# Local attention in blocks of 32 queries: paired transposes and values on array quarters

## The reference

```
def local_attention(q, k, v):            # window w = 32, 16 heads of 64
    bq, bk, bv = (t.reshape(b, h, n // w, w, d) for t in (q, k, v))
    bk2, bv2 = look(bk), look(bv)        # each block with the one before it
    mask = (it < jb) | (it > jb + w) | (jb == -1)
    sim = einsum('bhwie,bhwje->bhwij', bq, bk2) * 8.0
    sim = where(mask, -max, sim)
    return einsum('bhwij,bhwje->bhwie', softmax(sim, -1), bv2)

def attn_layer(x, Wqkv, qs, ksc, Wo):
    q, k, v = split(x @ Wqkv, 3, -1)
    q, k = l2norm(q) * qs, l2norm(k) * ksc    # then rotary, with scales
    return local_attention(q, k, v) @ Wo
```

## Time and profile before

| | |
|---|---|
| time, median of 3 runs | 5304.71 us (5301.19 to 5307.71) |
| span of the profiled execution | 5297.4 us, first to last instruction |
| time of the profiled execution itself | not listed apart from the three runs |
| instructions | 148317 |
| TensorE, VectorE, ScalarE, GpSimd busy | 88%, 76%, 69%, 50% |
| mean granted clock of TensorE | 0.957 of full speed |
| DMA, mean | 54 GB/s |

### The profile page before, as it was taken

One profiled execution on the slowest core, in us unless ns is written; L12 is line 12 of the kernel. 1 busy time (PEld: TensorE's weight loads), 2 busy tenths in 40 slices (PEclk: granted clock), 3 DMA queues, 4 the chain that ended last, 5 costly groups with the idle time before them and its releaser, 6 DMA issues. The chain is left out here.

```text
span 5297.4 us, 148317 instructions
## 1 busy us (share of the span) xinstructions
PE 4675.9 (88%) x45796; PEld 2897.7 (55%) x45796; DVE 4003.6 (76%) x8097; ACT 3636.0 (69%) x11780; POOL 2657.4 (50%) x2108
## 2 busy tenths in 40 slices
PE   5999999698898998989989767989989989899897
PEld 1333332366565665656656544665656656566565
DVE  7888886587786877868778546878868778687785
ACT  1777777586785876858768514867858778587684
POOL 3000000465665666656656404656656566566564
PEclk6999999899999999999999977999999999999998
DMA  0000000222222222222222302222222222222223
GB/s 13 1 2 1 2 1 1 85 59 72 59 59 77 59 71 60 59 77 59 64 66 60 83 7 85 59 73 59 57 78 59 72 62 57 77 60 69 65 56 93
DMA packets 332305, 288.20 MB, mean 54 GB/s; under 512 B 149102, under 2 KB 290964, under 8 KB 329748
## 3 DMA queue, kind: packets, MB, share of 16 engines
q1 hardware_dynamic: 331028, 281.93, 20.6%
q10 hardware_dynamic: 768, 0.02, 0.0%
HBM read 100.42 MB, written 30.41 MB: 25 GB/s over the span
## 5 line engine op out<-in xcount | busy, mean ns | idle before, releaser
L929 POOL TENSOR_TENSOR g_rn<-g_ss,g_minus_half 128x8 f32<-128x8 f32 x384 | 636.8, 1658 | 299.7 <-DVE g_ss L1077 297.0
L929 POOL TENSOR_TENSOR f_rn<-f_ss,f_minus_half 128x8 f32<-128x8 f32 x384 | 636.8, 1658 | 299.2 <-DVE f_ss L1077 295.9
L425 DVE TENSOR_REDUCE a_maxima<-a_max 128x1 f32<-128x512 f32 x1024 | 651.3, 685 | 148.4 <-PE a_max L539 142.2
L1003 ACT ACTIVATE f_ex<-f_bank,f_nmx 128x96 f32<-128x96 f32 x1536 | 501.5, 338 | 226.8 <-DVE f_nmx L1082 226.8
L1003 ACT ACTIVATE g_ex<-g_bank,g_nmx 128x96 f32<-128x96 f32 x1536 | 501.6, 338 | 226.6 <-DVE g_nmx L1082 226.6
L349 ACT ACTIVATE a_pex<-a_scores 128x512 f32<-128x512 f32 x1024 | 531.7, 607 | 159.6 <-PE a_scores L548 159.6
L934 POOL TENSOR_TENSOR f_qr<-f_t 128x512 f32<-128x512 f32 x384 | 488.4, 1272 | 268.8 <-DVE f_t L1100 268.8
L934 POOL TENSOR_TENSOR g_qr<-g_t 128x512 f32<-128x512 f32 x384 | 488.2, 1271 | 269.0 <-DVE g_t L1100 269.0
L1172 PE MATMUL g_bank<-g_wqkv,g_xT 128*128 128x512 f32 x768 | 407.2, 613 | 30.4 <-ACT g_xT L977 24.3
L1172 PE MATMUL f_bank<-f_wqkv,f_xT 128*128 128x512 f32 x768 | 406.4, 612 | 29.2 <-ACT f_xT L977 24.5
L1077 DVE TENSOR_REDUCE g_ss<-g_sq 128x8 f32<-128x512 f32 x384 | 263.1, 685 | 207.9 <-ACT g_sq L985 207.9
(11 more groups left out here) (244 smaller groups left out, 11909.8 us busy)
## 6 DMA issues: line engine op xcount, KB each, us to landing
f_vw<-f_vt SPq DMA_DIRECT2D x96, 384.0 KB, 4.3
g_vw<-g_vt SPq DMA_DIRECT2D x96, 384.0 KB, 4.3
f_vw<-f_vt SPq DMA_DIRECT2D x96, 256.0 KB, 3.5
g_vw<-g_vt SPq DMA_DIRECT2D x96, 256.0 KB, 3.5
f_vw<-f_vt SPq DMA_DIRECT2D x96, 128.0 KB, 2.3
g_vw<-g_vt SPq DMA_DIRECT2D x96, 128.0 KB, 2.3
f_wqkv<-in_f_Wqkv_dram SPq DMA_DIRECT2D x7, 1536.0 KB, 9.5
g_wqkv<-in_f_Wqkv_dram SPq DMA_DIRECT2D x7, 1536.0 KB, 9.3
```

The costliest lines, as they stand in the source:

```text
L425: dve.tensor_reduce(maxima[:, m // 4, m % 4:m % 4 + 1], ps_max[m % 3][:], AX.X, ALU.max).then_inc(dv_max, 1)
L929: pool.tensor_tensor(rn[:, b, :], ss[:, b, :], minus_half[:], ALU.pow).then_inc(pl_rn, 1)
L1003: last = act.activation(ex[:, b, u, :], ps_s[:, h, KEYS * jj:KEYS * jj + KEYS], ACT.Exp, bias=nmx[:, b, u:u + 1], accum_out=sm[:, b, u:u + 1])
```

## The change

Blocks have 32 queries (`BLK` = 32, `NB` = 4 of them in a tile) and 64 keys. The probabilities of two heads are then 128 columns, and one transpose turns both: the first head's keys come to partitions 0 to 63, the second's to 64 to 127. The values of the four blocks are done on quarters of the array (64 rows by 64 columns); the two row halves write different banks, so `ps_o` spreads over two banks and `ps_pT` moves into one of them. `vw` holds v of one head of each pair on partitions 0 to 63 and of the other on 64 to 127, for four blocks, and ten DMAs fill it. The mask is put in by four matmuls on quarters in place of two. On ScalarE the copy to `aT` moves from the end of the chunk to before the exponentials. TensorE's order within a chunk stays; its waits change: the transposes of `pn` also wait for the copy to `aT` of the chunk before, and the values wait for the copy of `pT` of the same chunk.

```diff
-BLK = 64
+BLK = 32
+NB = P // BLK
...
-        one = [bank(i) for i in range(6)]
+        one = [bank(i) for i in range(4)]
+        ps_po = bank(4, 2)
         ps_s = bank(6, 2)
...
-        ps_pT = banks[4]
-        ps_o = banks[5]
+        ps_pT = ps_po[:, 0, 0:2 * P]
+        ps_o = ps_po[:, :, 2 * P:3 * P]
...
-        vw = sb("vw", [P, 2, 2, INNER])
+        vw = sb("vw", [P, 2, NB, PAIRS // 2 * P])
...
-        pT = sb("pT", [P, 2, 4, P])
+        pT = sb("pT", [P, 2, 2, P])
...
-                    sp.dma_start(vw[0:32, p, 0, :], vt[96:128, 1 - p, :]).then_inc(ld_vw[p], 16)
-                    sp.dma_start(vw[32:96, p, 0, :], vt[0:64, p, :]).then_inc(ld_vw[p], 16)
-                    sp.dma_start(vw[0:96, p, 1, :], vt[32:128, p, :]).then_inc(ld_vw[p], 16)
+                    for jj in range(2):
+                        k, cols = KEYS * jj, slice(512 * jj, 512 * jj + 512)
+                        sp.dma_start(vw[k:k + WINDOW, p, 0, :], vt[P - WINDOW:P, 1 - p, cols]).then_inc(ld_vw[p], 16)
+                        sp.dma_start(vw[k + WINDOW:k + KEYS, p, 0, :], vt[0:BLK, p, cols]).then_inc(ld_vw[p], 16)
+                        for blk in range(1, NB):
+                            r = BLK * blk - WINDOW
+                            sp.dma_start(vw[k:k + KEYS, p, blk, :], vt[r:r + KEYS, p, cols]).then_inc(ld_vw[p], 16)
...
-                        act.copy(pT[0:KEYS, b, :, :], ps_pT[0:KEYS, :].rearrange("p (u q) -> p u q", u=4)).then_inc(act_pT, 1)
+                        act.copy(pT[:, b, :, :], ps_pT.rearrange("p (h q) -> p h q", h=2)).then_inc(act_pT, 1)
...
-                        act.copy(vt[:, q, 512 * half:512 * half + 512], ps_v[:]).then_inc(act_v, 1)
+                        by_pair = vt[:, q, :].rearrange("p (jj g c) -> p g jj c", jj=2, g=4)
+                        act.copy(by_pair[:, 2 * half:2 * half + 2, :, :],
+                                 ps_v[:].rearrange("p (g jj c) -> p g jj c", g=2, jj=2)).then_inc(act_v, 1)
                     if c == 1 and real(t + 1, 0, 0):
                         put_xT(L, t + 1, 1 - q)
+                    if real(t, c, 7):
+                        tj, g = t + (c - 7) // 4, (c - 7) % 4
+                        p = (q + (c - 7) // 4) % 2
+                        act.wait_ge(pe_o, upto(pe_o, L, n - 7))
+                        act.wait_ge(pe_Wo, upto(pe_Wo, L, tj - 2))
+                        act.copy(aT[:, p, 2 * g:2 * g + 2, :], ps_o).then_inc(act_aT, 1)
                     if real(t, c, 4):
...
-                    if real(t, c, 7):
...
-                        act.copy(aT[:, p, 2 * g:2 * g + 2, :], ps_o[:, 0:2 * P].rearrange("p (j q) -> p j q", j=2)).then_inc(act_aT, 1)
...
                         pe.wait_ge(dv_pn, upto(dv_pn, L, n - 6))
+                        pe.wait_ge(act_aT, upto(act_aT, L, n - 8))
                         pe.wait_ge(act_pT, upto(act_pT, L, n - 7))
-                        for u in range(4):
-                            last = pe.transpose(ps_pT[0:KEYS, P * u:P * u + P], pn[:, b, u, :], ident[:])
+                        for h in range(2):
+                            last = pe.transpose(ps_pT[:, P * h:P * h + P],
+                                                pn[:, b, 2 * h:2 * h + 2, :].rearrange("p u c -> p (u c)"), ident[:])
...
+                        pe.wait_ge(act_exp, upto(act_exp, L, n - 5)).then_inc(own["pe"], 1)
                         for h in range(2):
-                            if first:
-                                pe.matmul(ps_s[:, h, 0:2 * KEYS], ident_bf[:], mask_bf[:, 0, :], start=True, stop=False)
-                            else:
-                                r = slice(BLK * h, BLK * h + BLK)
-                                pe.matmul(ps_s[:, h, 0:2 * KEYS], twice_bf[r, :], mask_bf[r, 1, :], start=True, stop=False,
-                                          tile_position=(BLK * h, 0))
+                            r = slice(DH * h, DH * h + DH)
+                            for o in (slice(0, DH), slice(DH, P)):
+                                seen = 0 if first and o.start == 0 else 1
+                                pe.matmul(ps_s[o, h, 0:2 * KEYS], twice_bf[r, o], mask_bf[r, seen, :], start=True, stop=False,
+                                          tile_position=(DH * h, o.start))
                         for jj in range(2):
-                            for blk in range(2):
+                            for blk in range(NB):
...
-                        pe.wait_ge(act_pT, upto(act_pT, L, n - 7))
+                        if g == 0:
+                            pe.wait_ge(ld_vw[p], upto(ld_vw[p], L, tj >> 1, 160))
                         pe.wait_ge(act_aT, upto(act_aT, L, n - 8))
...
-                        for jj in range(2):
-                            j = 2 * g + jj
-                            for blk in range(2):
+                        turned = min(n - 6, STEPS - 1) if known else n - 6
+                        pe.wait_ge(act_pT, upto(act_pT, L, turned)).then_inc(own["pe"], 1)
+                        for blk in range(NB):
+                            qs = slice(BLK * blk, BLK * blk + BLK)
+                            for jj in range(2):
+                                k = slice(KEYS * jj, KEYS * jj + KEYS)
                                 for h in range(2):
                                     r = slice(DH * h, DH * h + DH)
-                                    at = P * jj + BLK * blk
-                                    last = pe.matmul(ps_o[r, at:at + BLK], vw[:, p, blk, P * j + DH * h:P * j + DH * h + DH],
-                                                     pT[:, 1 - b, 2 * h + jj, BLK * blk:BLK * blk + BLK], start=True, stop=True,
-                                                     tile_position=(0, DH * h))
+                                    at = P * g + DH * h
+                                    last = pe.matmul(ps_o[r, jj, qs], vw[k, p, blk, at:at + DH], pT[k, 1 - b, h, qs],
+                                                     start=True, stop=True, tile_position=(KEYS * jj, DH * h))
```

More of the change, by code:

```diff
@@ L63, in host_tables @@
     first = np.where(seen & (c[None, :] >= WINDOW), f(0), f(MASKED))
-    start = np.where(np.arange(P)[:, None] < BLK, first, rest)
+    start = np.where(np.arange(P)[:, None] % DH < BLK, first, rest)
     mask = np.stack([np.stack([m, m], 1) for m in (start, rest)], 1)
@@ L650, in bank @@
             return ctx.enter_context(nc.psum_tensor(f"{tag}_bank{i}", [P, n, 512], F32))
-        one = [bank(i) for i in range(6)]
+        one = [bank(i) for i in range(4)]
+        ps_po = bank(4, 2)
         ps_s = bank(6, 2)
-        banks = [t[:, 0, :] for t in one] + [ps_s[:, 0, :], ps_s[:, 1, :]]
+        banks = [t[:, 0, :] for t in one] + [ps_po[:, 0, :], ps_po[:, 1, :], ps_s[:, 0, :], ps_s[:, 1, :]]
         ps_qk = banks[0:2]
@@ L679, in local_stack @@
         ident = sb("ident", [P, P])
-        ident_bf = sb("ident_bf", [P, P], BF16)
         twice_bf = sb("twice_bf", [P, P], BF16)
@@ L724, in local_stack @@
         ld_r = [sem(f"ld_r{p}", 16 * NT // 2) for p in range(2)]
-        ld_vw = [sem(f"ld_vw{p}", 48 * NT // 2, 48) for p in range(2)]
+        ld_vw = [sem(f"ld_vw{p}", 160 * NT // 2, 160) for p in range(2)]
         ld_f = [sem(f"ld_f{p}", 16 * NF // 2) for p in range(2)]
```

24 lines of the change are left out of this document (8 added, 16 removed).

## The result

The changed kernel takes 5376.72 us (median of 4 runs, 5370.26 to 5382.93) against 5305.73 for the one before on the same chip: 1.0133 times the time before, 95% interval 1.0119 to 1.0148. The forecast was 5230, with a range up to 5365. It is slower by 71 us where about 75 less was forecast. The span of the profiled execution is 5378.5 us, before it was 5297.4: 81.1 more.

The account below looks back on a forecast made before the run. A ScalarE-VectorE loop paces chunks 0 to 2, then TensorE: 17.27 us a tile. New legs 3.64, 3.99, 2.64, 4.98 and 1.60 sum to 16.85; 180 x 0.42 = 76 us less gives 5230, range 5165 to 5365.

Parts of the forecast that it names:

- The loop from landing to landing: Ten vw DMAs and ScalarE's vt copy: 13.9 + 2.3 = 16.2 us a tile, under 16.85, so hidden by 0.7.
- 180 x 0.42: Whole kernel: 0.42 us saved a tile over 12 layers of 15 counted tiles, 76 us in all.
- DMA late: Rival: vw DMAs land after 4.3 us under queued issues, tile 18.2, +165 us, 5470 us; chance 10%.
- the count of 15 tiles for 16: Layer ends: first and last tiles lack stages, so 15 of a layer's 16 tiles were counted for the saving.
- Chunk 0 to 1: Steady tile, exponentials of chunk 0 to those of chunk 1: 3.64 us, was 3.86.
- Chunk 1 to 2: Steady tile, the same loop with kT's copy of 0.82: 3.99 us, was 4.20.
- To the values of chunk 3: Steady tile, from chunk 2's exponentials to the values of chunk 3: 2.64 us, was 2.47.
- Values to masks: Steady tile, TensorE from chunk 3's values to the next masks: 4.98 us, was 5.20, less one saving of 0.22.
- Masks to exps: Steady tile, from masks to exponentials: 0.60 + 0.74 + 0.26 = 1.60 us, was 1.54.
- better or worse cases: Steady tile: shorter handovers and values, 16.4 us, 5150, 12%; or waits eating the gain, 17.6 us, 5365, 15%.
- the old loop: ScalarE and VectorE loop pacing chunks 0 to 2; without aT 3.36 us from chunk 0 to 1, under the new loop's 3.64.
- TensorE by records: Rival, scores and values: 32 small records cost twice 16, tile 19.8 us, 5760; 5%. Milder form 17.6, 5365; 8%.

Follow-up runs that it names:

- prev_first: The changed kernel with the two DMAs that read the vt half overwritten next issued first, on a semaphore of their own: 5302.93 us, 0.9995 of before.
- drain_half: prev_first with the values of every pair's second head left out in tiles 16 and 17, while the layer drains: 5290.34 us, 0.997 of before.
- aT_early: The kernel before with only ScalarE's aT copy moved ahead of the exponentials: 5234.46 us, 0.9865 of before.
- pT_first: prev_first with ScalarE's pT copy put ahead of the square of the same chunk: 5227.0 us, 0.983 of before.
- ten_before: The kernel before with its three DMAs a tile cut into ten of the same bytes: 5320.29 us, 1.0029 of before.

## Why the prediction was wrong, and where it was right

**The step that failed** is "The loop from landing to landing ... 16.2, under 16.85: hidden, by 0.7", together with "180 x 0.42". The first holds in the steady tile and there alone: the vt copy is released by the DMA, and it costs nothing. In a layer's first tiles one issue of the ten takes up to 2.2 us for 0.6, and the tiles are shorter, since stages are still missing: where no vt copy is late, in prev_first, gaps 1 to 3 are 14.2, 15.3 and 16.4 us (medians), the first two under the 16.2 of my own loop. A margin of 0.7 was taken from one tile and used for all 180. The wait took 73 us (after against prev_first), 49 of them in gap 3 alone, 4.1 a layer for a copy held 1.8 to 3.9: the stop of TensorE that it makes and the low clock behind it are in that price. I had the case as a rival, "DMA late", but priced it by landing time in the steady tile; it came by issue time and in other tiles.

**The wrong side, too, is accounted for, though not all of it explained.** Spans: the DMA wait +73; the rest of the layer +48; the steady and late tiles -34; the early ones, without the wait, -11; the start +4. Sum +81. The second term that failed is the count of 15 tiles for 16, "the first and last of a layer lack stages": it costed the ends of the layers at nothing but fewer tiles, and without the DMA wait the kernel would still be level with before (prev_first, 0.9995) and not 75 us faster. Of the 48, 13 hang on the number of products in the drain (drain_half); aT_early's rest is also 10.2 above before, so some comes with the aT move. The others, with the low clock and the waits for the kT and pT copies there, are open.

**The steady sum was right, leg by leg.** Chunk 0 to 1: 3.72 (1501.69 less 1514.91 - 16.94) for 3.64. Chunk 1 to 2: 1505.70 - 1501.69 = 4.01 for 3.99. To the values of chunk 3: 2.68 for 2.64. Values to masks: 4.96 for 4.98. Masks to exps: 1.57 for 1.60. Exps with their reads 1.17 for 1.18, transposes 0.22, values 0.67, and the values start 0.14 after the pT copy ends where they wait, for 0.12. The tile came out 0.09 longer than summed, 16 us in 180 tiles. What I called better or worse cases did not happen there.

**The credit was in the wrong place.** The prediction said that the aT copy leaves the old loop "but makes a new one". It did not ask what the move is worth without the rest. It is worth 0.56 a tile (aT_early); all else in the change, put on top of it, makes the steady tile 0.22 worse. The smaller work of TensorE (1.29 us a tile) is paid for with the wait for the pT copy, which the shared bank forces, 0.60 + 0.17 + 0.60 in the tile, and the pT copy stands behind a square that is less urgent (pT_first is 69.5 us of span shorter than prev_first). My expectation for aT_early repeated the error: it took the values' end to lie behind the place of the exps, but TensorE's values of a chunk start before ScalarE has done its copies, and aT waits 0.21 and 0.61 in two chunks of the tile, in the place where ScalarE waited 0.26 to 0.69 ahead of the exps before.

**TensorE by records.** The rule that I weighed, from the Trainium skill, "TensorE: Matmul & The Clock Gate", section "Wait — 56ns, not 53.3ns?", would have 32 records take 0.8 us, an estimate from its 25 ns. The 32 scores take 0.46 and the 32 values 0.67, tail and all. The trace doesn't agree with it for matmuls that go to different parts of the array in turn. With the positions kept at four, 16 more records added 0.17 (0.56 to 0.73), 11 ns each. (The rival's 18.5 us a tile would be 5526 by the prediction's own sum, not 5540.)

## What to carry to other kernels

A margin read in the steady tile holds only there: before calling a transfer hidden, look for the shortest tile and the slowest issue, and give each copy a wait for just those DMAs that read what it overwrites. When a change needs a move in some engine's order, time the move alone; here it was worth more than what it was made for. And after a buffer is made to share a bank, look at what stands ahead of the copy that frees it: with the copy one place ahead, before the square, the time fell by 1.7% (0.9995 to 0.983), and one place further it rose by 2.9% (to 1.0111).

## What the runs showed of the hardware

A DMA issue on SyncE takes 0.6 us, but some take 1.0 to 2.2: 2 of 576 issues of `vw` before, 48 of 1920 in ten_before, 67 of 1920 after. All of these 67 fill tiles 1 to 4 and 13 to 15 of a layer, so they are issued in code that is written out, in the first pass of the loop or at the start of its second.

The trace has a DMA queue (q8) of the kind `instruction`, which moved 5.73 MB after and 4.16 before, in packets of 16 KB. In all 67 slow issues such a packet comes to its end while the issue is under way, and in 53 of them the issue ends 0.36 to 0.39 us later. Of the other 1853 issues 97 overlap one. In prev_first it is 82 of 82 and 105 of 1838, in ten_before 48 of 48 and 62 of 1872, before 2 of 2 and 33 of 574. So the times say that a slow issue waits for the fetching of instructions; no run was made to change it.

TensorE has stops of its own, like the 2.24 us inside a group of 32 matmuls with nothing to wait for, also in written-out code. Of the five over 1 us in such groups in the changed kernel four overlap a packet of that queue, which ends 1.3 to 1.5 us before TensorE goes on, and one overlaps none. That it is the same cause there is a guess.

A single stall of TensorE can cost more than its length: 1.7 us idle, and behind it a projection at 1.91 us for 1.02, with a granted clock of 0.70 over 9 us. With the wait taken away (prev_first) that fall is gone in all twelve layers, and gap 3 is 4.1 us shorter. I had not expected 153 us less of TensorE's time to go with a lower mean clock, 0.934 for 0.957.
